# Values taken from the normalised input in fp32r and multiplied by the attention weights, with the small steps of norms two and three done together

## What is computed

```python
x = x + attn(layernorm(x), W_qkv, b_qkv, W_proj, b_proj)
x = x + xattn(layernorm(x), ctx, ctx, ...)
x = x + ffn(layernorm(x), W1, b1, W2, b2, scale)

def attn(x, W_qkv, b_qkv, W_proj, b_proj):
    q, k, v = split(einsum('bsd,de->bse', x, W_qkv) + b_qkv)
    a = sps_pro(einsum('bsd,btd->bst', q, k) * SCALE)
    a = softmax(a)
    out = einsum('bst,btd->bsd', a, v)
    return einsum('bsd,de->bse', out, W_proj) + b_proj
```

## Time and profile before

| what | us |
| --- | --- |
| median of 3 runs | 1894.96 |
| lowest and highest | 1893.61, 1895.69 |
| the profiled execution | 1895.91 |
| its span, first to last instruction | 1894.2 |
| PE busy | 1811.0 |
| DVE busy | 1457.2 |
| ACT busy | 1075.5 |

### The profile page before, as it was taken

One profiled execution on the slowest core, in us unless ns is written; L12 is line 12 of the kernel. 1 busy time (PEld: TensorE's weight loads), 2 busy tenths in 40 slices (PEclk: granted clock), 3 DMA queues, 4 the chain that ended last, 5 costly groups with the idle time before them and its releaser, 6 DMA issues.

```text
span 1894.2 us, 44279 instructions
## 1 busy us (share of the span) xinstructions
PE 1811.0 (96%) x14040; PEld 1358.6 (72%) x14040; DVE 1457.2 (77%) x4492; ACT 1075.5 (57%) x2440; POOL 335.6 (18%) x301
## 2 busy tenths in 40 slices
PE   5579999999999999999999999999999999999988
PEld 4457777777777777777777777777777777777766
DVE  6688777787877787877778787777887777878752
ACT  1355666555566655566655556665555665555552
POOL 2120221121122122012212102211211221220210
PEclk9789999999999999999999999999999999999999
DMA  4110111111111111011111111111101111110000
GB/s 121 24 37 26 24 47 47 47 47 33 29 32 47 47 47 46 25 24 46 47 47 47 36 34 25 47 47 47 47 27 24 44 47 47 47 39 32 14 26 25
DMA packets 205743, 75.57 MB, mean 40 GB/s; under 512 B 150273, under 2 KB 205186, under 8 KB 205714
## 3 DMA queue, kind: packets, MB, share of 16 engines
q1 hardware_dynamic: 205714, 75.21, 15.6%
HBM read 53.93 MB, written 16.78 MB: 37 GB/s over the span
## 4 chain that ended last, share of the span: by engine, by line
PE 87%; ACT 6%; DVE 4%; issue 2%; DMA 0%; SPq 0%; DVEq 0%; ACTq 0%
PE UA L1378 17%; PE UB L1378 5%; PE UB L1320 5%; PE UA L1320 5%; PE PV L1320 5%; PE TA L1345 3%; PE TB L1456 3%; PE GT L1388 3%; PE TA L1456 3%; ACT QKs L697 3%; PE TA L1285 3%; PE TA L1186 3%; PE TB L1186 3%; PE TB L1320 2%; ACT hs_all L707 2%; PE UA L1396 2%
## 5 line engine op out<-in xcount | busy, mean ns | idle before, releaser
L1378 PE MATMUL UA<-W2f,hs_all 128*128 128x256 f32 x1536 | 350.8, 381 | 11.1 <-ACT hs_all L707 8.0
L1378 PEld LDWEIGHTS UA<-W2f,hs_all 128*128 128x128 f32 x1536 | 286.5, 190 | 76.6 <-ACT hs_all L707 23.7
L1039 DVE TENSOR_TENSOR C<-qT,QKs 128x512 f32<-128x512 f32 x256 | 171.2, 689 | 95.1 <-ACT qT L716 85.3
L601 POOL TENSOR_TENSOR Ng<-HT,gnw_b 128x256 f32<-128x256 f32 x128 | 99.8, 779 | 789.6 <-ACT HT L729 789.6
L580 POOL TENSOR_TENSOR xg<-x,gnb_b 128x1024 f32<-128x1024 f32 x32 | 84.1, 2627 | 683.0 <-ACT ot L671 646.0
L1378 PE MATMUL UB<-W2f,hs_all 128*128 128x256 f32 x512 | 115.8, 379 | 0.0
L615 ACT ACTIVATE lv<-ve 128x4 f32<-128x4 f32 x95 | 19.0, 200 | 163.6 <-DVE ve L834 163.6
L1378 PEld LDWEIGHTS UB<-W2f,hs_all 128*128 128x128 f32 x512 | 95.0, 190 | 11.7
L697 ACT ACTIVATE QKs<-DD 128x512 f32<-128x512 f32 x64 | 38.3, 598 | 105.4 <-PE DD L1345 105.4
L968 DVE COPY acs<-DD 32x256 f32<-32x256 f32 x32 | 13.2, 412 | 97.1 <-PE DD L1281 97.1
L1345 PEld LDWEIGHTS TA<-xn2T,ctxT 32*128 32x128 f32 x512 | 63.3, 190 | 26.8 <-issue 24.3
(11 more groups left out here) (328 smaller groups left out, 5086.1 us busy)
## 6 DMA issues: line engine op xcount, KB each, us to landing
xin<-x SPq DMA_DIRECT2D x32, 512.0 KB, 3.5
blocks<-ctx SPq DMA_DIRECT2D x256, 64.0 KB, 1.9
vc<-ctx SPq DMA_DIRECT2D x32, 512.0 KB, 3.5
out<-ot SPq DMA_DIRECT2D x32, 512.0 KB, 2.9
Ev<-xn SPq DMA_DIRECT2D x512, 1.0 KB
hs_all<-L_ffn_W SPq DMA_DIRECT2D x4, 512.0 KB, 8.7
E<-xn SPq DMA_DIRECT2D x128, 16.0 KB
T<-tok SPq DMA_DIRECT2D x128, 8.0 KB, 1.7
```

What stands on the lines that cost most here:

```text
L601: pool.tensor_tensor(Ng[:, b, :].rearrange("p (k n) -> p k n", k=2), HT[:, b % 2, :, 0:P], gnw_b[:, :].rearrange("p (k n) -> p k n", k=2), ...
L1039: dve.tensor_tensor(C[:, b % 2, :, half], dx[hf].rearrange("p (h i) -> p h i", h=HEADS), QKs[:, b, :, half], ALU.mult)\
L1378: ins = pe.matmul(OB[b][:, 0:D], hs_all[:, k, b * S:(b + 1) * S], W2f[:, k, :], start=(i == 0), stop=(i == KH - 1))
```

## The change

Three things are changed.

First, the self-attention. The matrix `Wvp` gets four more columns, which all hold the weights of the old `wrow`, so it has 260 (`DV`). In the step in which xn1 of the coming group is made, `project_v` computes V = xn1 Wvp for its four sequences, and `project_q` the queries, both as three products in fp32r (`xn1h`, `xn1l`; the split weights `Wvh`, `Wvl`, `Awh`, `Awl`). ACT copies the four results to `V` (`keep_v`), and `row_terms` reads its column 256. In the next step `attend` multiplies the attention weights by V, one matmul a sequence, where `mix`, two copies on ACT (`px_copy`) and `values` stood. ACT makes `xn1h` with two more copies out of PSUM, DVE makes `xn1l` with two subtractions (`xn1_low`), which stand between L1131's product and the sum x3. To make room, xn1 shares memory with `blocks`, y with `band_a`, PT with `sc`, and xn1's halves with those of xn3.

Second, PE's order and its banks. `down(0)` goes to TA, `down(2)` to GT; `down(1)` is split in two halves and stands where `mix` and `values` stood, with `adapt(1)`; `down(2)` is split around `turn_xn1`, whose results go to QQ and DD. `project_v` and `project_q` stand after it, and `down(3)` last, still in UA and still behind `o_out(1)`.

Third, the norms. The statistics of x2 are taken before those of x3, and the moments, the root and the scale of norms two and three are done once for both (128x8 instead of twice 128x4). ACT's one root for them stands after the copies of the queries.

The core of the diff:

```diff
-                def down(b):
-                    if b == 1 or b == 3:
-                        pe.wait_ge(ot_ok.h, ot_ok.at(it, (b + 1) // 2))
-                    elif b == 2:
-                        pe.wait_ge(HT_ok.h, HT_ok.at(it, G))
-                    for i, k in enumerate(ORDER):
+                def down(b, part=range(KH)):
+                    if part[0] == 0 and b == 0:
+                        pe.wait_ge(QKs_ok.h, QKs_ok.at(it, 7))
+                    elif part[0] == 0 and b == 2:
+                        pe.wait_ge(emT_ok.h, emT_ok.at(it, 1))
+                    elif part[0] == 0 and b == 3:
+                        pe.wait_ge(ot_ok.h, ot_ok.at(it, 2))
...
+            def project_v(it):
+
+                pe.wait_ge(xn1h_ok.h, xn1h_ok.at(it, KD))
+                pe.wait_ge(dexp_ok.h, dexp_ok.at(it, 2 * G))
+                pe.wait_ge(HT_ok.h, HT_ok.at(it, G))
+                for b in range(G):
+                    for w in (Wvh, Wvl):
+                        for k in range(KD):
+                            pe.matmul(VB[b][:, 0:DV], xn1h[:, k, b * S:(b + 1) * S], w[:, k, :],
+                                      start=(w is Wvh and k == 0), stop=False)
+                pe.wait_ge(xn1l_ok.h, xn1l_ok.at(it, KD))
+                for b in range(G):
+                    for k in range(KD):
+                        ins = pe.matmul(VB[b][:, 0:DV], xn1l[:, k, b * S:(b + 1) * S], Wvh[:, k, :],
+                                        start=False, stop=(k == 1))
+                    ins.then_inc(v_mm.h, 1)
+
+            def project_q(it):
+
+                pe.wait_ge(x2_ok.h, x2_ok.at(it, G))
+                pe.wait_ge(xn1h_ok.h, xn1h_ok.at(it, KD))
+                pe.wait_ge(xn1l_ok.h, xn1l_ok.at(it, KD))
+                for m in range(KD):
+                    for w, xt in ((Awh, xn1h), (Awl, xn1h), (Awh, xn1l)):
+                        for k in range(KD):
+                            ins = pe.matmul(TAB[m][:, :], w[:, k, m * P:(m + 1) * P], xt[:, k, :],
...
-                def mix(m):
-                    pe.wait_ge(PT_ok.h, PT_ok.at(it, 1))
-                    for b in range(G):
-                        ins = pe.matmul(TAB[m][:, b * S:(b + 1) * S], xn1[:, b, m * P:(m + 1) * P],
-                                        PT[:, b * S:(b + 1) * S], start=True, stop=True)
...
+                    ins = pe.matmul(XB[b][:, (b % 2) * D:(b % 2) * D + D], PT[:, b * S:(b + 1) * S], V[:, b, 0:D],
+                                    start=True, stop=True)
...
+            def row_terms(it):
+
+                dve.wait_ge(v_ok.h, v_ok.at(it, 0))
+                dve.tensor_scalar(rowterm[:, :], V[:, :, D], c0[:, 0:1], None, ALU.add).then_inc(rowterm_ok.h, 1)
...
+                if coming:
+                    xn1_low(it)
+                if cross:
                     dve.wait_ge(xg_ok.h, xg_ok.at(it, 1))
...
+                if own:
+                    dve.wait_ge(x2_ok.h, x2_ok.at(it, G))
+                    stats = ln_stats(1, x2)
+                if cross:
                     dve.wait_ge(x3_ok.h, x3_ok.at(it, 1))
-                    for b in range(G):
-                        ins = dve.bn_stats(stat[2][:, b, :], x3[:, b, :])
-                    link(ins)
-                    ln_moments(2, link)
+                    stats = ln_stats(2, x3)
+                if own or cross:
+                    link(stats)
+                    ln_moments(norms, norms_ve_ok, link)
                 if ffn:
                     o_out(1)
```

More of the change, by code:

```diff
@@ L40 @@
 KD = D // P
+DV = D + 4
 HID = 1024
@@ L1214, in _ @@
                 ins.then_inc(s_set_pe, 1)
-            for ec in range(KD):
-                pe.matmul(DD[:, 0:D], bB[:, 0, ec, :], wT[:, 0, ec, :], start=(ec == 0), stop=(ec == 1))
+            for m in range(KD):
+                for ec in range(KD):
+                    pe.matmul(QQ[:, KD + 1 + m:KD + 2 + m], wT[:, 0, ec, m * P:(m + 1) * P],
+                              bcol[:, 2 + ec:3 + ec], start=(ec == 0), stop=(ec == 1))
             for ec in range(KD):
@@ L1233, in _ @@
             ins.then_inc(s_set_pe, 1)
-            pe.wait_ge(s_set_v, V_WT + 4)
-            for m in range(KD):
-                for k in range(KD):
-                    project_q(-1, m, k)
+            pe.wait_ge(s_set_v, V_WT + 6)
+            project_q(-1)
+            pe.wait_ge(s_set_v, SETUP_V)
+            project_v(-1)
             def turn_w1():
                 pe.wait_ge(s_load, 16 * LOADS)
-                pe.wait_ge(s_set_v, SETUP_V)
+                pe.wait_ge(v_ok.h, v_ok.at(-1, G))
                 for i in range(4):
@@ L1481, in step @@
                     decay(2, 1)
-                if own:
-                    mix(0)
+                if ffn:
+                    down(1, range(0, 4))
                 if cross:
                     turn_h(1)
-                if own:
-                    mix(1)
-                if cross:
                     decay(3, 0)
@@ L1491, in step @@
                     decay(3, 1)
+                if ffn:
+                    down(1, range(4, KH))
                 if own:
-                    values(0)
+                    attend(0)
+                    attend(1)
                 if cross:
                     turn_h(2)
-                if own:
-                    values(1)
+                if ffn:
+                    adapt(1)
                 if cross:
@@ L1500, in step @@
                 if own:
-                    values(2)
-                    values(3)
+                    attend(2)
+                    attend(3)
                 if isinstance(it, int) and it == 0:
@@ L1510, in step @@
                 if ffn:
-                    down(1)
-                    adapt(1)
+                    down(2, range(0, 4))
                 if coming:
-                    turn_xn1(it)
+                    turn_xn1(it, (QQ, DD))
                 if ffn:
-                    down(2)
+                    down(2, range(4, KH))
                     adapt(2)
                 if coming:
-                    project_q(it, 0, 0)
-                    project_q(it, 0, 1)
-                    project_q(it, 1, 0)
-                    project_q(it, 1, 1)
+                    project_v(it)
+                    project_q(it)
                 if ffn:
```

228 lines of the change are left out of this document (117 added, 111 removed).

## The result

The changed kernel takes 1898.92 us (median of 17 runs, 1896.87 to 1901.42), the kernel before 1894.88 (17 runs on the same chips, 1892.45 to 1899.62). The ratio is 1.0020, with a 95% interval of 1.0013 to 1.0027: slower by 4.0 us. A second comparison on another occasion gave 1.0030 (1.0018 to 1.0042). The forecast was 1903, slower by 8: the direction holds and the time lies in the range, but the loss is half of what was summed.

What follows compares the result with a forecast made beforehand. PE, busy 96% of the span, was taken as the bound. Steps of 55.95 us for 55.87 gave +2.3, the ends 2.6 + 0.9 + 2.4: +8.2 on 1895.91, 1904.1; the median 0.95 below, 1903 us, range 1888 to 1918.

Steps and rivals of the forecast that it cites:

- What bounds the kernel, and the mechanism: Middle steps: PE bounds; DVE's late `o_out(1)` makes `down(3)` wait for `ot_ok`, taking the place of the matmuls saved.
- Matmul time: PE's matmuls in a step: 8.6 us removed against 7.6 added, so 1.0 us less; V costs 3.07 us.
- rival (a): `down(3)` not held, PE keeps its gain: step 55.07 us, 0.8 less; 1878 us in all; chance 0.15.
- Rival (b): V's 260-column matmuls bound by weight loads: V 4.5 us, +0.92 us a step, 1930 us; chance 0.10.
- From the transposes to pv(1): Transposes of xn3 to `pv(1)`: `down(0)` starts about 0.35 us earlier, given back at `pv(1)`; 30.44 us against 30.49.
- From turn_h(3) to the transposes: Step's stretch up to xn3's transposes: `o_out(1)` ends at 12.23, `down(3)` starts at 12.28; 16.28 us against 16.42.
- From pv(1) to turn_h(3): Step's last stretch: `mix` and `values` out, 5.6 us of 256-column instructions in; 9.23 us against 8.96, +0.27.
- The ends: First and last steps: start +2.6 us, step 1 +0.9, steps 31 and 32 with the end +2.4.

Runs made afterwards that it cites:

- The pads on PE and on DVE: Changed kernel with four more 260-column matmuls on PE: 1901.10 us; changed kernel with one more statistics instruction on DVE ahead of `o_out(1)`: 1907.30 us.
- the moved instruction: Changed kernel with DVE's `o_out(1)` moved ahead of `head_sums(3)`: 1882.19 us, ratio to before 0.9932.
- the second profile of the changed kernel: The changed kernel run and profiled once more without an edit: 1901.95 us, ratio to before 1.0030.

## Why the prediction was half right

**What bounds the kernel, and the mechanism: right.** The wait for `ot_ok` took the place of the matmuls saved, in the 29 full steps, 0.66 us long in the mean where 0.5 to 1 was forecast. The pads on PE and on DVE and the moved instruction show it as the cause, and not as a companion.

**Matmul time: right.** V was put at 3.07 us and took 2.99, so 0.125 a matmul of 260 columns, next to the 0.128 taken; it started at 5.42 (5.6). The first scores leave ACT at 42.54 (42.3). PE's own step, once nothing holds it, is 54.88 to 54.94, where rival (a) had 55.07.

**Rival (b), the loads as the bound: excluded.** A load of V is still 0.188 us long in its records, and the matmuls stand 0.125 apart, so they overlap. The prediction's estimate for a pair whose load and matmul do not overlap, worked out from the Trainium skill, "TensorE: Matmul & The Clock Gate", section LDWEIGHTS, was 218 ns; the trace does not bear it out, it has 125. By the prediction's own chain for (b) that pair would also have given some 1950 us and not 1944; nothing else rests on it.

**From the transposes to pv(1): right.** 30.42 against 30.44, and `down(0)` without a wait, 21.72 after the transposes in place of 22.08. The 0.36 is given back at `pv(1)`, as forecast. The profile puts the wait ahead of `pv(1)`'s weight load down to ACT's copy `HT` and not to DVE's products, in both kernels; both end at 1109.75 here, so which of the two holds it the trace does not tell. The loads of `vc` and E are not waited for. ACT waits 1.8 us a step for the store of the output, which the forecast had moving later; the first layer's GELUs come no later for it (11.70 after the transposes, 11.68 before).

**From turn_h(3) to the transposes: the term that failed.** The prediction put "`xn1_low`, two passes like the 1.30 at 1022.97, next start 1.25 later, and the statistics of x2, 1.35" ahead of `o_out(1)`, 2.60 us in all on top of the 9.20 of the earlier trace rows. `o_out(1)` starts at 11.54: 2.34 more, not 2.60. Each new piece breaks up a pair in which the second reads what the first wrote, and so 0.12 and 0.13 us come back (Ng to its neighbour 1.14 in place of 1.26, x3 to its neighbour 1.13 in place of 1.26). The rest is small and cancels: the new pieces themselves take 1.21 and 1.32 (put at 1.25 and 1.35), and the way to Ng and the moments of both norms at once are 0.04 longer each. `down(3)` started at 12.02, not 12.28, and the transposes at 16.01, not 16.28. This is 0.27 a step, 7.8 us over 29 steps: more than the 4.2 us by which the whole change was put too high (8.2 against 4.0).

The Trainium skill gives a reason that fits in "Perfetto Trace Analysis", section "DVE / Act Engine Instruction": the reported time of an instruction runs until its write is acknowledged and its semaphore is pushed, while the next one may begin its prefetch once the execution has ended. The trace agrees: an independent instruction starts 0.08 before the end reported for the one ahead of it (1067.97 + 1.22 against 1069.11), a dependent one 0.03 after it (1072.64 + 1.23 against 1073.90).

**From pv(1) to turn_h(3): short by 0.15.** 9.38 against 9.23, 4.4 us over 29 steps. By its starts, one gap was not in the sum: from the decay matmul at 1112.88 to `pv(2)` at 1113.37 it is 0.49, where 0.31 stood before. The trace names no releaser for it, but the code has `pv(2)` wait for DVE's products of its sequence, and the rows fit. First DVE and PE of the kernel before, then of the changed one:

```profile
1052.99 1.28 DVE L1039 TENSOR_TENSOR C<-qT,QKs 128x512 f32<-128x512 f32 x2
1054.63 0.64 PE L1423 MATMUL PV<-C,vc 128*32 128x128 f32 x16
```

```profile
1111.94 1.28 DVE L1052 TENSOR_TENSOR C<-qT,QKs 128x512 f32<-128x512 f32 x2
1113.37 0.64 PE L1469 MATMUL PV<-C,vc 128*32 128x128 f32 x16
```

The products end at 1113.22 and `pv(2)` follows 0.15 later, and it is 0.14 or 0.15 in all 29 full steps; before, they had been over for 0.36. The products start 2.04 after `pv(1)`, where they started 1.85 after it; why they do was not tested. So the forecast had this stretch as PE's own, and DVE ends one gap in it.

The two errors have opposite signs, and 55.95 became 55.80. It is in part luck that the forecast's direction held: it had the middle steps 0.08 slower, they are 0.07 faster, and the kernel is slower by its ends alone.

**The ends: right in sum, not in their parts.** 5.9 forecast; 7.5 in the profile, 6.1 by medians. At the start xn2's first transposes come at 81.59, 5.4 later (forecast 5.0). Of this more than the 2.4 forecast comes back: `turn_h(3)` of step 1 starts at 111.54 for 110.85, only 0.7 later. Then the end of step 1 costs 4.5 and not 0.9: from there to the transposes of xn3 it takes 17.56 in place of 13.06. PE before, then PE and DVE now:

```profile
123.91 0.65 PE L1174 MATMUL QQ<-ident,xn 128*128 128x128 f32 x4 [0.86 <-ACT qT L649]
```

```profile
129.10 1.11 PE L1192 MATMUL QQ<-ident,xn 128*128 128x128 f32 x4 [3.88 <-DVE xn L852]
```

```profile
126.31 0.17 DVE L841 TENSOR_TENSOR nt<-rs 128x8 f32<-128x8 f32 x1 [3.02 <-ACT rs L619]
```

Step 1 has no second layer. PE stands still for 4.10 us ahead of V, which then takes 5.12 us in place of 2.99 (most of it at half clock), and the norms' one root stands on ACT behind the copies of the queries that follow V. The forecast named this order, the root behind those copies, as what would be late next, but in step 1, where nothing else holds PE, it gave 0.9 us without a working. In the kernel with the norms apart, where the root of norm three stands ahead of the copies, the same stretch takes 14.51; in the second profile of the changed kernel it takes 16.98. At the start of step 2 it is +5.2 (129.10 for 123.91) where 3.5 was summed, and step 2 then gives back 1.0. The waits of steps 31 and 32, forecast at 5 to 7, are 6.43 and 5.08, but the slow clock behind them costs 2.4 and 3.0, not 1.7, since most of `down(3)` runs at it. Against this, 3.6 of the 4.0 us lost in step 31 come back by the start of the next first layer (1809.87 for 1807.43, with 2.06 brought along), where half was forecast; of the 4.0 lost in step 32, 1.0 comes back by the end of the span.

**What I did not see.** The sum treated the norms' part as a cost, 1.35 us more ahead of `o_out(1)`. With the norms apart the changed kernel takes 1921.7: the merging is the part that pays, 22.7 us. And the forecast had rival (a) at 0.15 as something that might happen by itself; it was one instruction away. `adapt(1)`, which makes the input of `o_out(1)`, starts 2.07 us before `turn_h(3)` (1117.21 and 1119.28), and DVE stands 0.60 us for ACT just behind.

## What to carry to other kernels

When an instruction is put into a chain of another engine, its price is not its own length plus the old distances: between two dependent instructions an independent one was 0.12 us cheaper here than it looks, twice a step and over 29 steps 7 us, more than the 4 us that the change cost. Where a busy engine is to gain, look for the small instruction that releases it late, and ask how early its input is there: here moving one of 0.42 us was worth 17 us of time. And look at the few steps at the ends apart from the others: the 28 middle steps gained 2.1 us, the ends lost three times as much, and one wait on the last setup instruction was 4.6 of it.
